# Gate and up projections of a two-layer block: the last block of a pair in pieces over the tokens' chunks, the next pair's split beside it

## What is computed

```
def _L0_ffn_ref(x, w_gate, w_up, w_down):
    h = jax.nn.silu(jnp.einsum('bsh,hi->bsi', x, w_gate)) * jnp.einsum('bsh,hi->bsi', x, w_up)
    h_sparse = _sparsify_2to4(h)
    return jnp.einsum('bsi,ih->bsh', h_sparse, w_down)
x = x + jnp.tanh(g_ffn[0]) * _L0_ffn_ref(_layernorm(x, axis=-1), L0_ffn_w_gate, L0_ffn_w_up, L0_ffn_w_down)
```

## Time and profile before

| | |
|---|---|
| median of 3 runs | 2157.63 us (2154.73 to 2162.49) |
| the profiled execution's own time | 2155.77 us |
| its span | 2154.0 us |
| PE busy | 1963.9 us, 91% of the span |
| DVE busy | 1344.3 us, 62% |
| ACT busy | 1072.4 us, 50% |
| mean granted clock of TensorE | 0.967 of full speed |

### The profile page before, as it was taken

How to read it: one execution, slowest core, us unless ns; L and a number is a source line. 1 busy time by engine, 2 the same in 40 slices (tenths; PEclk the granted TensorE clock), 3 DMA queues, 4 the chain that set the end, 5 groups by cost and what they waited for, 6 DMA issues and landing times. The chain is left out here.

```text
span 2154.0 us, 33149 instructions
## 1 busy us (share of the span) xinstructions
PE 1963.9 (91%) x10498; PEld 1491.0 (69%) x10514; DVE 1344.3 (62%) x2408; ACT 1072.4 (50%) x2590; POOL 428.9 (20%) x515
## 2 busy tenths in 40 slices
PE   6999789999999999978998999999979978886898
PEld 5788667777777777756887778778768865554444
DVE  6777566666666666654342755555645437884886
ACT  3333356666656666653222312222324328984998
POOL 1111144444444444430000000000000001222111
PEclk9999899999999999999999999999989988997999
DMA  6776843333323240118443121112477422331121
GB/s 252 260 256 221 293 129 108 79 89 79 96 74 108 60 107 22 30 30 293 136 142 112 59 79 39 59 39 88 127 255 258 157 85 89 108 108 46 35 59 44
DMA packets 209016, 253.55 MB, mean 118 GB/s; under 512 B 12246, under 2 KB 158822, under 8 KB 202476
## 3 DMA queue, kind: packets, MB, share of 16 engines
q1 hardware_dynamic: 208876, 251.82, 36.7%
HBM read 151.10 MB, written 100.68 MB: 117 GB/s over the span
## 5 line engine op out<-in xcount | busy, mean ns | idle before, releaser
L966 ACT ACTIVATE at_prob<-at_S,at_bias,at_rq 128x384 f32<-128x384 f32 (+1 forms) x256 | 184.1, 731 | 142.9 <-DVE at_bias L1051 138.1
L1062 DVE TENSOR_TENSOR at_pt_lo<-at_PT,at_pt_hi 128x512 fp32r<-128x512 f32 x224 | 148.8, 688 | 92.3 <-ACT at_pt_hi L973 92.2
L835 POOL TENSOR_SCALAR at_prob<-at_prob,at_rsum 128x384 f32<-128x384 f32 (+1 forms) x256 | 160.3, 639 | 135.0 <-DVE at_rsum L1057 135.0
L1713 ACT ACTIVATE gu_silu<-gu_G 128x512 f32<-128x512 f32 x64 | 38.1, 596 | 245.3 <-PE gu_G L103 236.0
L1042 DVE TENSOR_REDUCE at_nmax<-at_S 128x1 f32<-128x384 f32 (+1 forms) x256 | 150.9, 617 | 9.5 <-PE at_S L885 5.5
L973 ACT ACTIVATE at_pt_hi<-at_PT 128x512 fp32r<-128x512 f32 x224 | 127.9, 604 | 53.8 <-PE at_PT L892 53.8
L892 PE MATMUL at_PT<-c_ident,at_prob 128*128 128x128 f32 x896 | 127.8, 277 | 21.1 <-DVE at_pt_lo L1062 20.8
L1750 DVE TENSOR_TENSOR gu_h<-gu_silu,gu_U 128x512 f32<-128x512 f32 x64 | 43.8, 686 | 151.6 <-PE gu_U L103 105.2
L824 POOL TENSOR_TENSOR at_q<-at_by_cos,at_by_sin 128x512 f32<-128x512 f32 x64 | 82.1, 1283 | 265.0 <-DVE at_by_sin L1034 152.5
L892 PEld LDWEIGHTS at_PT<-c_ident,at_prob 128*128 128x128 f32 x896 | 97.8, 140 | 50.9 <-DVE at_pt_lo L1062 46.5
L881 PE MATMUL at_S<-at_k_hi,at_q_hi 128*128 128x384 f32 (+1 forms) x256 | 113.2, 442 | 15.5 <-DVE at_q_lo L1067 11.5
(11 more groups left out here) (341 smaller groups left out, 5474.7 us busy)
## 6 DMA issues: line engine op xcount, KB each, us to landing
wide<-at_ot SPq DMA_DIRECT2D x64, 256.0 KB, 2.9
wide<-gu_h SPq DMA_DIRECT2D x64, 256.0 KB, 3.2
o_a<-wide SPq DMA_DIRECT2D x14, 1024.0 KB, 4.8
d_a<-wide SPq DMA_DIRECT2D x13, 1024.0 KB, 8.6
keys_hi<-kv_kt_hi SPq DMA_DIRECT2D x16, 512.0 KB, 3.3
keys_lo<-kv_kt_lo SPq DMA_DIRECT2D x16, 512.0 KB, 4.1
values_hi<-kv_v_hi SPq DMA_DIRECT2D x16, 512.0 KB, 4.7
values_lo<-kv_v_lo SPq DMA_DIRECT2D x16, 512.0 KB, 5.0
```

The source lines that it names most:

```text
L835: pool.tensor_scalar(prob[u % 2][:, h, 0:n], prob[u % 2][:, h, 0:n], rsum[:, s:s + 1], 1.0, ALU.mult, ALU.mult).then_inc(normed.sem, 1)
L966: act.activation(prob[u % 2][:, h, 0:n], S[h][:, 0:n], ACT.Exp, bias=bias[:, s:s + 1], scale=rq[u % 4][:, h:h + 1], accum_out=sums[:, s:s ...
L1062: dve.tensor_tensor(pt_lo[f % 4][:], bank_of("p", u, kb)[:], pt_hi[f % 4][:].bitcast(F32), ALU.subtract).then_inc(pt_done.sem, 1)
```

## The change

Only where another pair follows, block 15 takes another order. On PE both products are made chunk by chunk: for each k the three passes of the gate, then the three of the up product; behind the up passes of chunks 0, 1 and 2 a new counter `n_free` rises, and behind those of chunk 3 `G_full` and `U_full`. The waits for both banks stand ahead of the block. On ACT and DVE `split_n` of the next pair moves ahead of silu 15 and product 15; ACT's copy of chunk n waits for `n_free` of that chunk, and the last one for `U_full`.

```
--- before.py
+++ after.py
+        n_free = mem.counter("n_free", DC - 1)
...
+            def last_block(turn):
+
+                i = IC - 1
+                q, j = divmod(i, 4)
+                pe.wait_ge(w_ready, 2 * q + 2)
+                pe.wait_ge(*silu_done.at(turn, i - 1))
+                pe.wait_ge(*h_done.at(turn, i - 1))
+                for k in range(DC):
+                    for n, bank, full in (("g", G[i % 2], G_full), ("u", U[i % 2], U_full)):
+                        last = three_passes(pe, bank[:], [(w_hi[n][q][:, k, j, :], w_lo[n][q][:, k, j, :],
+                                                           n_hi[:, k, :], n_lo[:, k, :])],
+                                            start=(k == 0), stop=(k == DC - 1))
+                        if k == DC - 1:
+                            last.then_inc(full.sem, 1)
+                        elif n == "u":
+                            last.then_inc(n_free.sem, 1)
...
                     if more and i == IC - 1:
                         turn_xn(turn + 1)
+                        last_block(turn)
+                        continue
...
             def split_n(turn):
-                act.wait_ge(*U_full.at(turn, 0))
                 for n in range(DC):
+                    act.wait_ge(*(n_free.at(turn - 1, n + 1) if n < DC - 1 else U_full.at(turn, 0)))
                     act.wait_ge(*T_full.at(turn, n + 1))
...
             def body(turn, more):
                 for i in range(IC):
+                    if more and i == IC - 1:
+                        split_n(turn + 1)
                     act.wait_ge(*G_full.at(turn, i + 1))
...
-                if more:
-                    split_n(turn + 1)
                 sizes(turn, NC - 1)
...
             def body(turn, more):
                 for i in range(IC):
                     q, j = divmod(i, 4)
+                    if more and i == IC - 1:
+                        split_n(turn + 1)
                     product(turn, i)
...
-                if more:
-                    split_n(turn + 1)
                 for step in range(3):
                     choose(turn, NC - 1, step)
```

More of the change, by code:

```diff
@@ L1654, in _ @@
         def _(pe):
-            for s in (T_full, G_full, U_full):
+            for s in (T_full, G_full, U_full, n_free):
                 s.start(pe)
```

## The result

| | changed kernel | kernel before |
|---|---|---|
| median | 2132.4 us, 4 runs (2131.05 to 2135.47) | 2156.18 us, 4 runs (2149.67 to 2162.49) |
| the profiled execution's own time | 2131.05 us | 2155.77 us |
| its span | 2129.2 us | 2154.0 us |
| mean granted clock | 0.974 | 0.967 |

The ratio is 0.9898, with an interval of 0.9877 to 0.992. On another chip it was 0.9916 (0.9894 to 0.9938), 2134.4 against 2154.1 us.

The account below looks back on a forecast made before the run. The prediction took the stage to be bound by PE, except at pair ends, where PE waits for DVE's subtraction. It summed 11.9 + 4.4 - 1.3 = 15.0 us gained, forecasting 2141.6 us, range 2136 to 2149.

Parts of the forecast that it names:

- Term 1, the gap: At the three ends of a pair, PE's wait for DVE's subtraction goes: 12.62 us become 0.68, gaining 11.9 us.
- Term 2, the clock: Gate products behind the gaps run partly at the lower clock after PE idles; with no gap, 4.4 us are gained.
- The clock falls all the same: Rival: the gate products stay slow without the gap, so the 4.4 us remain: 2146.0 us, chance 0.07.
- Term 3, every chunk in time: In block 15, chunks 0 to 2 are split while PE works; chunk 3 is hidden by 0.5 us.
- Term 4, product 0 late: PE newly waits for the next pair's product 0 at block 2's up product: 0.42 us each end, 1.3 in all.
- Term 5, queues and banks: Pair 3's down load keeps 3.1 us of its 8.0 us margin; bank changes in block 15 cost at most 0.01 each.
- The branch back becomes visible: Rival: PE's two loop branches between pairs, until now beneath the wait, cost 5.8 us: 2147.4 us, chance 0.05.
- Alternating banks lowers the clock: Rival: block 15 in groups of three runs at 1.2 GHz, costing 15.1 us: 2156.7 us, no change, chance 0.04.
- Product 0 much later: Rival: ACT's and DVE's work behind the split slips 2 us at each end and lowers the clock: 2150.1 us, chance 0.08.
- the store: Rival: product 0 also waits until quarter 2's store has landed, making the kernel slower: 2171 us, chance 0.03.
- It doesn't do what it says: Rival: DVE is caught in another step and PE waits for chunk 0 as before: some 2156 us, chance 0.03.

Follow-up runs that it names:

- before_again: The kernel before, unchanged, run and profiled once more: 2152.45 us, ratio 0.9999.
- gap_awake_short: The kernel before with 17 small products that keep PE busy in the gap behind block 15 where a pair follows: 2147.74 us, ratio 0.9971.
- pe_order: The kernel before with only PE's block 15 in pieces; ACT and DVE keep their old order, copies wait for the whole block: 2152.37 us, ratio 1.0001.
- step_first: The changed kernel with DVE's step of quarter 2 moved ahead of the subtractions: 2132.48 us, ratio to the kernel before 0.9904.
- after_pause_b: The changed kernel with a chain of 75 small DVE writes between gate_up and the down stage: 2155.51 us, ratio to the kernel before 1.0004.

## Why the prediction was right or wrong: direction and mechanism held, the size did not

- **Term 1, the gap (11.9 us): right.** 12.62 us became 0.68.
- **Term 2, the clock (4.4 us): mechanism right, mis-sized.** This is the step that failed. It was read from one execution, in which the first of three equal gaps left the clock high, and 4.4 us was taken for what it costs in every execution; in before_again the same gap cost 4.45 - 2.72 = 1.7 us at that place. The term is 6.8 us in the trace of before_again and 6.4 us by gap_awake_short's time. That is 2.0 to 2.4 us more than forecast; pe_order's trace has 7.5 us with its up products. The rivals asked only whether the term could be smaller ("The clock falls all the same"), and no part of the range stood for a larger one.
- **Term 3, every chunk in time: right**, at the forecast times within 0.05 us.
- **Term 4, product 0 late (0.42 us at each end): right.** Idle 0.18, 0.25 and 0.25 us where 0.29 was summed; 1.2 us in all where 1.3 was. The slower start behind a wait was part of it. The hidden magnitudes, with 0.3 us of cover, are what step_first ran into.
- **Term 5, queues and banks: right** for the banks (pe_order). Of the down load in pair 3 only its effect was read: the wait of PE for silu there was 0.80 us before, 0.33 in before_again, 1.05 in the changed kernel and 0.37 in its second trace, which is no clear cost.
- **The base.** The sum was made against 2155.77 and 2157.63 us. Medians of 26 and 23 runs are 2153.7 and 2154.1; the first trace held a second attention stage 8 us longer than the next one's. The forecast time was thus 2.7 us too high at its base. This is the second thing that was mis-sized: the sum leaned on one profiled execution and three times.
- **What the two do not explain.** With 2153.9 as the base and 11.9 + 6.6 - 1.2 = 17.3 as the gain it would be 2136.6 us. Measured were 2134.4 (6 runs) and 2132.4 (4 runs). So of the 9.2 us between the forecast 2141.6 and 2132.4, 2.7 are the base, 2.3 the terms, nearly all of it the clock's, and 4.2 have no cause that was found; these alone carry the time from inside the range to below it. Against 2134.4, 2.2 are open. The traces of the stage itself agree with the terms: `gate_up` took 404.05, 404.55 and 406.36 us with the old gaps (pe_order is the third) and 388.02 and 387.71 in the changed kernel, 17.1 us less in the mean. What is open thus lies outside the stage. The upper ends of the intervals, 0.9938 and 0.992, stand for 2140.5 and 2136.7 from that base and do not exclude that it is chance. All three traces with the change and no pause have the short second attention stage (mean 208.7), while the six with the old gaps, shorter ones or filled ones have 208.5 to 216.5 (mean 210.8), 2.1 us more; with a stage that varies on its own, and 211.68 in after_pause_b, that is too few to call a cause.

The rivals. *The branch back becomes visible*: refuted, the steps from start to start at the two branches are 0.23 us. Instruction fetches in the DMA view of the changed kernel, 1258 to 1458 us (queue, packets, MB, share):

```profile
q14 instruction: 3, 0.02, 0.1%
```

In the same execution the attention loop's branch stops PE as in the earlier trace rows:

```profile
612.74 0.40 PE L103 MATMUL at_O<-at_pt_lo,at_v_hi 128*128 128x512 f32 x1
615.43 0.44 PE L881 MATMUL at_S<-at_k_hi,at_q_hi 128*128 128x384 f32 x1 [2.30 <-issue]
```

The rule of the Trainium skill (Runtime: NRT & Kernel Launch, section Instruction fetch mechanics), that a taken branch waits where its target is no longer held, agrees with both rows; how much PE holds, no run here shows. *Alternating banks lowers the clock*: refuted by 0.23 us from start to start in block 15 (rows of 0.39 us, the length at the full clock) and by pe_order's time. The Trainium skill's case of it (TensorE: Matmul & The Clock Gate, section A second HAM failure mode: psum-queue depth-cycling) rests on small pauses between groups; changing banks every three matmuls made none here. *The clock falls all the same*: refuted by the gate products of 2.72 us. *Product 0 much later* and *the store*: product 0 started at Z + 13.34 and waited for no store. *It doesn't do what it says*: refuted by the copies.

## What to carry to other kernels

An engine that another waits for at a loop's end, and that idles just before, can often be given its work in pieces: put its work for the waiter ahead of work that can wait, and then have the shared buffer freed piece by piece. The first half, the order on ACT and DVE alone, brought 11 to 13 of some 20 us. Before moving more work off such a path, look at what is hidden behind that work: in step_first, taking a 2.3 us step off the path brought 0.27 us, since the magnitudes had been hidden behind it by 0.3 us only. Price a gap on TensorE with the lower clock behind it, and read that price from two or three traces, or measure it by filling the gap with small products. A clock dip behind two of three gaps in one trace does not say that the third place is safe.

## What the runs showed of the hardware that I had not expected

- The same 4.18 us gap at the same place left the clock high in one execution and lowered it in others: gate and up product behind it took 5.57 us, and 7.16 (before_again) and 7.20 (pe_order). Where it fell, it could fall behind the restart: in before_again the first three matmuls of pair 1 still ran at the full clock, and the fourth, at 1269.50, took 0.63 us.
- A 128x128 fp32 product stands in the trace as two matmuls, 0.11 us from start to start, 0.22 in all.
- A branch back can cost nothing (0.23 us from start to start) and in another loop of the same program 2.3 to 2.7 us of idle.
- One stage of unchanged code varied from 208.5 to 216.5 us between executions, a third or more of what the whole change brings, and its long execution had the lower granted clock (0.66 and 0.74 against 0.91 and 1.00). What sets it off was not found.
